# Two LayerNorms of a graph block: normalising moved from VectorE to ScalarE, the attention vectors folded into the weights, the attention table stored block by block

## What is computed

```
xn = layernorm(x)                                    # first norm: (x - mean) / sqrt(var + eps)
h  = xn @ w1.T + b1                                  # then batch statistics of h, ReLU, w2, w_gcn
x1 = x + gcn(h, edges) + linear_attention(xn)
xf = layernorm(x1)                                   # second norm
g  = xf @ W_gat                                      # 16 columns: 4 heads of 4
a_src, a_dst = (g * att_src).sum(-1), (g * att_dst).sum(-1)
agg = softmax over each node's edges of leaky_relu(a_src[src] + a_dst[dst]), weighting g[src]
out = x1 + sum over 2 of 4 experts (gate from agg) of gelu(xf @ W1[e] + b1[e]) @ W2[e] + b2[e]
```

## Time and profile before

| | us |
|---|---|
| median of 3 runs (lowest to highest) | 4793.2 (4790.67 to 4804.6) |
| the profiled execution | 4790.88 |
| its span, first to last instruction | 4789.0 |
| VectorE busy in the span | 2604.3 (54%) |
| ScalarE busy | 880.5 (18%) |
| TensorE busy | 3688.3 (77%) |
| GpSimd busy | 3085.5 (64%) |

### The profile page before, as it was taken

How to read it: one execution, slowest core, us unless ns; L and a number is a source line. 1 busy time by engine, 2 the same in 40 slices (tenths; PEclk the granted TensorE clock), 3 DMA queues, 4 the chain that set the end, 5 groups by cost and what they waited for, 6 DMA issues and landing times. The chain is left out here.

```text
span 4789.0 us, 44151 instructions
## 1 busy us (share of the span) xinstructions
PE 3688.3 (77%) x13162; PEld 2442.9 (51%) x13162; DVE 2604.3 (54%) x6218; ACT 880.5 (18%) x1738; POOL 3085.5 (64%) x3019
## 2 busy tenths in 40 slices
PE   3667888888798998787887564799999999700377
PEld 1355555455555555555555354466666666500255
DVE  5946776666666556666666364134334333312476
ACT  2653222222100000000000011222222223200232
POOL 2515777777776776777777500777777777777630
PEclk7989999999887998777677655899999999955689
DMA  6645444444454664333333765444444334322588
GB/s 178 188 98 152 129 130 132 130 130 130 125 154 132 182 177 131 89 91 89 92 91 89 71 193 137 132 114 113 138 115 113 117 106 138 97 63 63 114 209 196
DMA packets 262492, 606.63 MB, mean 127 GB/s; under 512 B 88254, under 2 KB 144369, under 8 KB 256893
## 3 DMA queue, kind: packets, MB, share of 16 engines
q0 software_dynamic: 124496, 304.94, 24.1%
q1 hardware_dynamic: 137772, 299.02, 22.2%
HBM read 447.85 MB, written 155.88 MB: 126 GB/s over the span
## 5 line engine op out<-in xcount | busy, mean ns | idle before, releaser
L1039 POOL DMA_INDIRECT g_rows<-table,gcn_srcT x1664 | 1758.2, 1057 | 568.0 <-issue 485.7
L1109 PE MATMUL g_ps<-g_rows,g_hot 128*125 128x256 f32 x3328 | 1064.3, 456 | 337.4 <-issue 229.6
L1902 POOL DMA_INDIRECT n_rows<-gtab,so_own x1122 | 1095.6, 977 | 341.9 <-issue 341.9
L1394 DVE TENSOR_TENSOR acc<-acc,g_ps 125x256 f32 x1664 | 696.4, 419 | 691.6 <-PE g_ps L1109 565.6
L1109 PEld LDWEIGHTS g_ps<-g_rows,g_hot 128*125 128x125 f32 x3328 | 685.8, 223 | 622.8 <-issue 410.0
L1842 PE MATMUL p_ph<-f_xfT,f_w 128*128 128x500 f32 x1344 | 576.7, 585 | 64.2 <-DMA f_xfT<-xfT_d 64.2
L1848 PE MATMUL p_py<-f_w,f_hh 128*125 128x256 f32 x2688 | 590.4, 379 | 0.0
L1848 PEld LDWEIGHTS p_py<-f_w,f_hh 128*125 128x125 f32 x2688 | 504.5, 188 | 101.1 <-issue 27.4
L2045 DVE TENSOR_TENSOR p_ob<-p_py,p_xb 125x512 f32<-125x512 f32 x168 | 115.6, 691 | 699.0 <-PE p_py L1848 698.6
L1842 PEld LDWEIGHTS p_ph<-f_xfT,f_w 128*128 128x128 f32 x1344 | 256.4, 191 | 348.6 <-issue 343.5
L2073 ACT ACTIVATE f_hh<-p_ph,f_b 128x500 f32<-128x500 f32 x336 | 221.4, 677 | 616.4 <-PE p_ph L1842 616.1
(11 more groups left out here) (338 smaller groups left out, 4329.8 us busy)
## 6 DMA issues: line engine op xcount, KB each, us to landing
o_d<-p_ob SPq DMA_DIRECT2D x21, 1920.0 KB
z_ob<-o_d SPq DMA_DIRECT2D x21, 1920.0 KB
g_rows<-table,gcn_srcT POOLq DMA_INDIRECT x1664, 3.0
n_rows<-gtab,so_own POOLq DMA_INDIRECT x1122
gout<-n_o SPq DMA_DIRECT2D x33, 408.0 KB, 2.5
xnT_d<-a_xnT SPq DMA_DIRECT2D x25, 500.0 KB
m_area<-xnT_d SPq DMA_DIRECT2D x25, 500.0 KB, 3.8
qT_d<-m_area SPq DMA_DIRECT2D x25, 500.0 KB, 3.1
```

Source lines behind the costliest of these rows:

```text
L1039: pool.indirect_dma_start(out=rows[:, g % RING, j], out_offset=None, in_=K.table, in_offset=bass.IndirectOffsetOnAxis(ap=K.gcn_srcT[:, 4 * ...
L1109: mm = pe.matmul(ps[q, p % 4, b], hot[:, g % 4, 2 * j + b], rows[:, g % RING, 2 * j + b], start=True, stop=True, skip_group_check=True)
L1394: dve.tensor_tensor(a, a, ps[q, p % 4, b], ALU.add).then_inc(add_s, 1)
L1902: pool.indirect_dma_start(out=rows[:, c % 3, j], out_offset=None, in_=K.gtab, in_offset=bass.IndirectOffsetOnAxis(ap=K.gat_src[:, c * W + ...
```

## The change

In `first_half` the clearing of `gtab` and its tile are gone. Of the four tiles of a block VectorE normalises two and ScalarE two: ScalarE computes Identity(x * r + off), r the reciprocal of the root and off = -mean * r, which VectorE makes in one more small operation. ScalarE does this right after the root of a block, ahead of the copies of the block before.

In `gather_mix` six operations in `lists` turn node numbers into row numbers, since a node's row in `gtab` is now (n mod 125) * 100 + n div 125: the four rows that one partition makes in a block lie side by side.

`second_norm` is written out without hardware loops, with three buffers for `pre` and x1. ScalarE does all four normalisations. The attention vectors are multiplied into the weights once (`prod`, `fold`), so that the product has 24 columns and gives whole table rows. ScalarE copies them into `wide`, 128 columns wide, whose rest GpSimd has cleared once, and SyncE stores each block's rows as 2,048 bytes per partition. The tail after the last block is gone.

```diff
@@ -458,7 +456,8 @@
                 def load(k):
                     if k >= 3:
-                        sp.wait_ge(xn_s, (k - 2) * SUB)
+                        sp.wait_ge(xn_s, (k - 2) * (SUB // 2))
+                        sp.wait_ge(xna_s, (k - 2) * (SUB // 2))
                     rows_in_two(sp, xin[:, k % 3], A.x[k * BN:(k + 1) * BN].rearrange("(j p) f -> p j f", p=TN), x_in[k % 3])
 
@@ -477,9 +476,6 @@
                 rows_in_two(sp, raw[:, 0], A.src.rearrange("(p c) -> p c", p=c), src_s)
 
-                sp.wait_ge(blank_s, 1)
-                sp.dma_start(K.gtab.rearrange("(t p) f -> p t f", p=TN)[:, :, TROW:TWIDE],
-                             blank[q].unsqueeze(1).to_broadcast([TN, NT, TWIDE - TROW])).then_inc(blank_s, 16)
                 for k in range(NB):
                     if k + 3 < NB:
@@ -512,7 +507,8 @@
             def _(pe):
                 def turn(k):
-                    pe.wait_ge(xn_s, (k + 1) * SUB)
+                    pe.wait_ge(xn_s, (k + 1) * (SUB // 2))
+                    pe.wait_ge(xna_s, (k + 1) * (SUB // 2))
                     if k:
                         pe.wait_ge(xnT_s, k * KC)
@@ -565,6 +561,15 @@
                     act.activation(rs[q, k % 2, :, 1], rs[q, k % 2, :, 0], ACT.Sqrt).then_inc(root_s, 1)
 
+                def normalise(k):
+                    s = k % 2
+                    act.wait_ge(off_s, k + 1)
+                    if k >= 2:
+                        act.wait_ge(turned, (k - 1) * KC)
+                    for j in range(SUB // 2, SUB):
+                        act.activation(xn[q, s, j], xin[q, k % 3, j], ACT.Identity, bias=off[q, s, j:j + 1],
+                                       scale=rs[q, s, j, 0:1]).then_inc(xna_s, 1)
+
                 def inside(g):
                     act.wait_ge(got[g % DEEP], 64 * (g // DEEP + 1))
@@ -579,11 +584,13 @@
 
                 root(0)
+                normalise(0)
                 act.wait_ge(w_s, 16 * 5)
                 act.wait_ge(node_s, 4)
                 for k in range(NB):
                     if k + 1 < NB:
                         root(k + 1)
+                        normalise(k + 1)
                     if k >= 2:
                         act.wait_ge(stored[k % 2], 16 * (k // 2))
@@ -624,9 +631,11 @@
                     dve.reciprocal(rs[q, s, :, 0], rs[q, s, :, 1]).then_inc(rec_s, 1)
                     dve.wait_ge(rec_s, k + 1)
+                    dve.scalar_tensor_tensor(off[q, s], mv[q, s, :, 0], -1.0, rs[q, s, :, 0], ALU.mult, ALU.mult
+                                             ).then_inc(off_s, 1)
                     if k >= 2:
                         dve.wait_ge(turned, (k - 1) * KC)
-                    for j in range(SUB):
+                    for j in range(SUB // 2):
                         dve.tensor_scalar(xn[q, s, j], xin[q, k % 3, j], mv[q, s, j, 0:1], rs[q, s, j, 0:1],
                                           ALU.subtract, ALU.mult).then_inc(xn_s, 1)
@@ -1587,6 +1595,12 @@
                     then(dve.tensor_scalar(K.gat_head[:, 0:1], high[:, 0:1], -128.0, None, ALU.add))
                     yield
+                    for at, of in ((K.gat_head[:, 0:1], odd[:]), (K.gat_src, K.opens.bitcast(I32))):
+                        then(dve.tensor_scalar(of, at, 1.0 / TN, 0.5 / TN - 0.5, ALU.mult, ALU.add))
+                        then(dve.tensor_scalar(at, at, float(NT), None, ALU.mult))
+                        yield
+                        then(dve.scalar_tensor_tensor(at, of, float(1 - TN * NT), at, ALU.mult, ALU.add))
+                        yield
                     then(dve.memset(col, 1.0))
                     then(dve.tensor_tensor_scan(col, col, col, -1.0, ALU.add, ALU.bypass))
@@ -1665,165 +1679,172 @@
...
+        RING = 3
+        pre = m.sb("c_pre", [P, RING, SUB, D])
+        x1 = m.sb("c_x1", [P, RING, SUB, D])
+        wide = m.sb("c_wide", [P, 2, SUB, TWIDE])
+        by_part = K.gtab.rearrange("(p k j) f -> k p (j f)", p=TN, j=SUB)
...
+                def load(k):
+                    if k >= RING:
+                        sp.wait_ge(x1_s, (k - RING + 1) * SUB)
+                    rows_in_two(sp, pre[:, k % RING], K.pre_d[k], in_p[k % RING])
+                sp.dma_start(wg[:, :, 0:GW], A.W_gat.rearrange("(c p) o -> p c o", p=P)).then_inc(w_s, 16)
                 for n, a in enumerate((A.att_src, A.att_dst)):
+                    sp.dma_start(att[:, n], a.rearrange("(o h) e -> o (h e)", o=1).to_broadcast([P, GW])).then_inc(w_s, 16)
+                for k in range(RING):
+                    load(k)
+                for k in range(NB):
+                    sp.wait_ge(xf_s, (k + 1) * SUB)
+                    rows_in_two(sp, K.x1_d[k], x1[:, k % RING], out_1[k % RING])
+                    if k + RING < NB:
+                        load(k + RING)
+                    sp.wait_ge(xfT_s, (k + 1) * KC)
+                    sp.dma_start(K.xfT_d[k], xfT[:, k % 2]).then_inc(out_f[k % 2], 16)
+                    sp.wait_ge(row_s, k + 1)
+                    rows_in_two(sp, by_part[k], wide[:, k % 2].rearrange("p j f -> p (j f)"), out_g[k % 2])
+                for s in range(RING):
+                    sp.wait_ge(out_1[s], 32 * ((NB + RING - 1 - s) // RING))
                 for s in range(2):
-                sp.wait_ge(S["trow"], 1)
-                sp.dma_start(K.gtab.rearrange("(t p) f -> p t f", p=TN)[:, :, 0:TROW], trow[0:TN]).then_inc(S["out"], 16)
-                sp.wait_ge(S["out"], 16)
+                    sp.wait_ge(out_f[s], 16 * ((NB + 1 - s) // 2))
+                    sp.wait_ge(out_g[s], 32 * ((NB + 1 - s) // 2))
+            @block.gpsimd
+            def _(pool):
+                pool.memset(wide[:], 0.0).then_inc(clear_s, 1)
             @block.vector
             def _(dve):
+                def statistics(k):
+                    r, s = k % RING, k % 2
+                    dve.wait_ge(in_p[r], 32 * (k // RING + 1))
+                    if k >= RING:
+                        dve.wait_ge(out_1[r], 32 * (k // RING))
                     for j in range(SUB):
                         t = k * SUB + j
+                        dve.scalar_tensor_tensor(x1[q, r, j], K.acc[q, t], K.dinv[q, t:t + 1], pre[q, r, j], ALU.mult, ALU.add
+                                                 ).then_inc(x1_s, 1)
                     for j in range(SUB):
+                        dve.wait_ge(x1_s, k * SUB + j + 1)
+                        dve.bn_stats(st6[q, s, j], x1[q, r, j]).then_inc(st_s, 1)
+                    if k >= 2:
+                        dve.wait_ge(xf_s, (k - 1) * SUB)
                     for j in range(SUB):
+                        dve.wait_ge(st_s, k * SUB + j + 1)
+                        dve.bn_aggr(mv[q, s, j], st6[q, s, j]).then_inc(mv_s, 1)
+                    dve.wait_ge(mv_s, (k + 1) * SUB)
+                    dve.tensor_scalar(rs[q, s, :, 0], mv[q, s, :, 1], EPS, None, ALU.add).then_inc(eps_s, 1)
+                def scales(k):
+                    s = k % 2
+                    dve.wait_ge(root_s, k + 1)
+                    dve.reciprocal(rs[q, s, :, 0], rs[q, s, :, 1]).then_inc(rec_s, 1)
+                    dve.wait_ge(rec_s, k + 1)
+                    dve.scalar_tensor_tensor(off[q, s], mv[q, s, :, 0], -1.0, rs[q, s, :, 0], ALU.mult, ALU.mult
+                                             ).then_inc(off_s, 1)
+                statistics(0)
+                dve.wait_ge(w_s, 16 * 3)
+                for a in range(2):
+                    dve.tensor_tensor(prod[:, a], wg[:, :, 0:GW], att[:, a].unsqueeze(1).to_broadcast([P, KC, GW]), ALU.mult
+                                      ).then_inc(fold_s, 1)
+                dve.wait_ge(fold_s, 2)
+                for a in range(2):
+                    dve.tensor_reduce(wg[:, :, GW + a * GH:GW + (a + 1) * GH],
+                                      prod[:, a].rearrange("p c (h e) -> p c h e", h=GH), AX.X, ALU.add).then_inc(fold_s, 1)
+                for k in range(NB):
+                    if k + 1 < NB:
+                        statistics(k + 1)
+                    scales(k)
             @block.scalar
             def _(act):
+                def roots(k):
+                    act.wait_ge(eps_s, k + 1)
+                    act.activation(rs[q, k % 2, :, 1], rs[q, k % 2, :, 0], ACT.Sqrt).then_inc(root_s, 1)
+                def normalise(k):
+                    s = k % 2
+                    act.wait_ge(off_s, k + 1)
+                    if k >= 2:
+                        act.wait_ge(turned, (k - 1) * KC)
+                    for j in range(SUB):
+                        act.activation(xf[q, s, j], x1[q, k % RING, j], ACT.Identity, bias=off[q, s, j:j + 1],
+                                       scale=rs[q, s, j, 0:1]).then_inc(xf_s, 1)
+                def copies(k):
+                    s = k % 2
+                    if k >= 2:
+                        act.wait_ge(out_f[s], 16 * (k // 2))
                     for c in range(KC):
+                        act.wait_ge(turned, k * KC + c + 1)
```

(35 more changed lines are left out.)

131 lines of the change are left out of this document (15 added, 116 removed).

## The result

The changed kernel takes 4900.3 us, median of four runs (4893.9 to 4904.1), against 4793.4 for the kernel before in the same comparison: a ratio of 1.0219, 95% interval 1.0201 to 1.0237. It is slower, as forecast, but by 107 us and not by 38; the time lies above the range. The profiled execution has a span of 4898.4 us.

The account below looks back on a forecast made before the run. Bounds seen: a 45.17 us gap behind the clearing, VectorE in the first half, a round trip through memory in the second norm. Sum 4790.9 + 89.1 - 45.2 - 6 + 0 = 4828.8, stated as 4831 against the median; range 4788 to 4874.

Parts of the forecast that it names:

- the clearing goes: First half: VectorE's 45.17 us of idle time go with the table's clearing; gain between 40 and 46.
- two normalisations move: First half: VectorE has 0.5 us less per block and sets the pace at 6.8; a gain of 6 us.
- the lists: Mix: six more VectorE operations taken as nothing, since gathers set the pace; 4.4 us without that cover.
- the second norm: Whole stage: 30.1 us, 21 rounds of 13.55 and 20.7 make 335.4, so 89.1 more than the present 246.3.
- the ring of one block per trip: Second norm: SyncE's and ScalarE's orders allow one block per round trip through transfer, VectorE and ScalarE, 13.55 us.
- the prediction's own sign of it: First half: needing over 7.5 us per block in the changed profile would show the forecast wrong.
- The end given for the case, a loss of 16: First half: if the slow product sets every block, 0.8 us lost over 20 blocks.
- Transfer: Second norm: table rows, x1 store and load, up to the load's landing, take 6.3 us a round; between 4.3 and 8.1.
- a rival at 17%: Second norm: the turned block's store shares the burst, transfer 8.1, round 15.2 us, 35 more, kernel 4866; chance 17%.
- VectorE's long by 0.4: Second norm: VectorE's x1 operations, statistics, reciprocal and offset take 4.2 us of each round.
- ScalarE's right to 0.1: Second norm: ScalarE's four activations at 1.70, two copies, the rows and the way between engines take 3.05 us a round.
- no ring: Second norm: three buffers hide the round trip, stage 36 us shorter, kernel 4706; chance 6%.

Follow-up runs that it names:

- first norm on VectorE: The changed kernel with the first norm's four normalisations back on VectorE, the clearing still out: 4867.0 us, ratio 1.015 to the kernel before.
- lists alone: The kernel before with only the six list operations added in the mix: 4797.7 us, ratio 1.0018 to the kernel before.
- ring broken: The changed kernel with SyncE storing block k-1's table rows behind turned block k in the second norm: 4747.5 us, ratio 0.991 to the kernel before.
- late store: The changed kernel with SyncE storing the turned block only once the load ahead of it has landed: 4869.0 us, ratio 1.0181 to the kernel before.

## Why the prediction was wrong in size

| step of the prediction | forecast | measured | from |
|---|---|---|---|
| the clearing goes | -45.2 | -45.3 | G, first norm on VectorE |
| two normalisations move | -6 | +31.1 | G, changed less first norm on VectorE |
| the lists | 0 | +9 (3 to 14) | lists alone |
| the second norm | +89.1 | +113.1 | X to N |
| sum | +38 | +108 | the runs: +107 |

The direction and the mechanism that decides it were right: the ring of one block per trip is there, and both ways of getting two blocks into a trip take 150 us off.

**The step that failed most** is the choice in "two of four normalisations move": "the granted clock in this stretch is 0.88, nearer to 2.4 than to 1.2 GHz, so I take VectorE's 6.8". The loop was written down correctly, and its two values, 6.4 or 8.1 us, were near (6.95 and 8.4 to 8.6; left out were the reciprocal and the offset, and the two activations took 1.09 us and not 0.84, in all some 0.5). But the clock of 0.88 was that of a kernel in which VectorE sets the pace and a slow product costs nothing. Once the loop is the pace, each slow product is paid in full, and the clock in the changed kernel is not the one of before: 0.80 from 100 to 160 us, where it had been 0.90, with a product of 5.1 to 5.3 us in every round; the prediction's own sign of it, over 7.5 us per block, came with 8.4 and 8.6. The end given for the case, a loss of 16, was also too small: it took 0.8 us over 20 blocks, the loop against the present 7.30. Against the run with the first norm on VectorE it was 1.1 over 24 rounds, 26 us; the first copies came 3.4 us later, and behind the last ones another 1.7 went by: 31.1. In the execution with the ring broken, which kept the higher level for twelve rounds, the part still cost 11 us (358.6 to 347.3): nine of its other twelve rounds took 8.4 us and more, and its first copies came as late.

**Transfer.** "Above: the store of the turned block ... shares the engines with it, 1.75 MB: 8.1" was near the value that came, 7.9 (7.7 in the mean), and I had made it a rival at 17%; but its reason holds for only about half of what was missing, as the run with the late store shows. The term of 6.3 was short by 1.6 us, VectorE's long by 0.4, ScalarE's right to 0.1 (its four activations took 2.07 us and not the 1.70 of the earlier trace rows, but overlapped the copies): together 1.3 us in the round shown and 1.1 in the mean, over 21 rounds 23 us, against the 24 that the stage is over the forecast. The Trainium skill (DMA: Bandwidth & Descriptors, section Anatomy of one DMA) would have given 4.9 us for this burst, as an estimate, by a fit to transfers that GpSimd issues. The burst is SyncE's; it took 6.9 by itself and 7.9 with the store beside it, so here the measurement decides against that estimate.

**The lists** were costed at nothing, since gathers set the pace, with a bound of 4.4 that counted the operations. They measured 3 to 14 us: the gathers themselves wait for TensorE where the lists run, 28.0 us for 15.7, and the granted clock there is lower; the 0.43 us that VectorE stands idle behind each step are the smaller part.

**The range** left room of 11 and 16 us for the first norm, beside a forecast and two rivals that all took the same 6.8 us of VectorE. A case "TensorE's loop becomes the pace" was an end of a term and not a rival with its own sum; with the slower ring it would have been 4869 + 22 = 4891 by the prediction's own figures. (8.1 + 4.2 + 3.05 is a round of 15.35, 38 us more, so that rival comes to 4869 and not to the 4866 that it was given.)

The rival "no ring" (4706) states what the change is worth without that wait: with the normalisations of the first norm behind the copies and the ring broken, lists and three buffers kept, the run took 4703. Its second norm is 36 us shorter than before, as that rival had it, though the round trip is not hidden but carries two blocks.
